# Graph attention layer: the values as two fp16 parts scaled per feature, in three products

## What is computed

```python
q = x @ wq.T + bq; k = x @ wk.T + bk; v = x @ wv.T + bv
q2, k2, v2 = (heads of q @ wiq.T + biq, k @ wik.T + bik, v @ wiv.T + biv)
mask = full(-inf); mask[src, dst] = softplus(w)[edge_type - 1]; # diagonal set where empty
scores = einsum('hnd,hmd->hnm', q2, k2) / 8 + mask
out = einsum('hnm,hmd->hnd', softmax(scores), v2)
return layernorm(x + (out @ wo.T + bo))
```

## Time and profile before

| | |
|---|---|
| median of 3 runs | 282.12 us (281.9 to 282.89) |
| the profiled execution | 282.69 us, span 280.9 us |
| TensorE, VectorE, ScalarE, GpSimd busy | 274.3, 174.6, 153.5, 137.1 us |
| value matmuls (L1025) | 240, busy 21.0 us |
| v2 stage ends, first attention step begins | 138.6 us |
| mean granted TensorE clock | 0.999 of full speed |

### The profile page before, as it was taken

One profiled execution on the slowest core, in us unless ns is written; L12 is line 12 of the kernel. 1 busy time (PEld: TensorE's weight loads), 2 busy tenths in 40 slices (PEclk: granted clock), 3 DMA queues, 4 the chain that ended last, 5 costly groups with the idle time before them and its releaser, 6 DMA issues.

```text
span 280.9 us, 5139 instructions
## 1 busy us (share of the span) xinstructions
PE 274.3 (98%) x1674; PEld 252.6 (90%) x1674; DVE 174.6 (62%) x425; ACT 153.5 (55%) x288; POOL 137.1 (49%) x123
## 2 busy tenths in 40 slices
PE   8999999999999999999999999999999999999992
PEld 8999999999999998888899989889898988787891
DVE  4879976765765676233506687857676577810472
ACT  5973343244244235233318989877879787933221
POOL 2000644565635555533697286483837466497000
PEclk9999999999999999999999999999999999999999
DMA  7949866274474335966404589795867849590032
GB/s 263 341 155 345 290 213 202 98 219 154 122 252 149 91 139 175 350 242 197 153 17 149 108 212 148 228 216 130 228 126 204 163 154 180 166 215 3 9 139 79
DMA packets 51921, 49.31 MB, mean 176 GB/s; under 512 B 41056, under 2 KB 41920, under 8 KB 51776
## 3 DMA queue, kind: packets, MB, share of 16 engines
q1 hardware_dynamic: 49792, 47.63, 58.4%
q0 software_dynamic: 1680, 0.62, 1.1%
q10 hardware_dynamic: 432, 0.85, 0.8%
HBM read 37.44 MB, written 2.21 MB: 141 GB/s over the span
## 4 chain that ended last, share of the span: by engine, by line
PE 98%; DVE 1%; ACT 0%; issue 0%
PE bank L928 24%; PE bank L919 19%; PE bank L921 19%; PE bank L920 19%; PE bank L1025 7%; PE bank L1007 5%; PE bank L944 3%; PE bank L937 1%; ACT res L606 0%; DVE stats L893 0%; DVE res L892 0%; DVE mean_var L895 0%; ACT std L601 0%; DVE scratch L623 0%; DVE rstd L898 0%
## 5 line engine op out<-in xcount | busy, mean ns | idle before, releaser
L387 POOL DMA_INDIRECT mask_cells<-scratch x48 | 53.8, 1120 | 72.1 <-DMA mask_cells<-scratch 29.6
L441 ACT ACTIVATE w_hi<-w_raw 128x1024 fp32r<-128x1024 f32 x49 | 51.5, 1053 | 22.2 <-PE bank L928 19.6
L349 POOL TENSOR_TENSOR w_lo<-w_raw,w_hi 128x1024 fp32r<-128x1024 f32 x17 | 40.8, 2404 | 39.9 <-DVE plane_lo_odd L826 30.4
L919 PE MATMUL bank<-x_hi,w_hi 128*128 128x384 f32 x176 | 58.8, 334 | 0.0
L920 PE MATMUL bank<-x_lo,w_hi 128*128 128x384 f32 x176 | 58.8, 334 | 0.0
L921 PE MATMUL bank<-x_hi,w_lo 128*128 128x384 f32 x176 | 58.8, 334 | 0.0
L633 DVE TENSOR_TENSOR w_lo<-w_raw,w_hi 128x1024 fp32r<-128x1024 f32 x31 | 37.9, 1225 | 16.6 <-ACT w_hi L441 15.6
L484 ACT ACTIVATE h_hi<-bank,bcol 128x384 f32 (+1 forms) x24 | 14.0, 582 | 55.4 <-PE bank L921 52.7
L919 PE MATMUL bank<-h_hi,w_hi 128*128 128x384 f32 x128 | 43.8, 342 | 0.0
L921 PE MATMUL bank<-h_hi,w_lo 128*128 128x384 f32 x128 | 42.8, 335 | 0.0
L920 PE MATMUL bank<-h_lo,w_hi 128*128 128x384 f32 x128 | 42.8, 334 | 0.0
(11 more groups left out here) (99 smaller groups left out, 443.1 us busy)
## 6 DMA issues: line engine op xcount, KB each, us to landing
w_raw<-weights SPq DMA_DIRECT2D x53, 512.0 KB
shared<-key_rows SPq DMA_DIRECT2D x6, 512.0 KB
shared<-start SPq DMA_DIRECT2D x5, 320.0 KB, 6.3
res<-x_rows SPq DMA_DIRECT2D x1, 1536.0 KB
out<-res SPq DMA_DIRECT2D x6, 256.0 KB, 2.2
mask_cells<-scratch POOLq DMA_INDIRECT x48
shared<-start ACTq DMA_DIRECT2D x2, 320.0 KB, 5.2
mask_cells<-mask SPq DMA_DIRECT2D x1, 576.0 KB, 6.0
```

The costliest lines, as they stand in the source:

```text
L349: nc.gpsimd.tensor_tensor(lo, w_raw[:, s, cols], hi.bitcast(F32), ALU.subtract)\
L387: nc.gpsimd.indirect_dma_start(out=mask_cells, out_offset=bass.IndirectOffsetOnAxis(ap=cell[:, c:c + 1], axis=0), in_=cell_value[:, c:c + ...
L441: nc.scalar.activation(w_part(t, s, slice(0, F))[0], w_raw[:, s, :], ACT.Copy).then_inc(w_hi_done, 1)
L919: pe.matmul(out_ps, w_hi[:, s, cols], moving_hi, start=(k == 0), stop=False)
```

## The change

The values are held as two fp16 parts instead of three bf16 parts, and the products are three: high plane by high and low part, low plane by high part. So that fp16 holds them, each feature (column of v2) is scaled: in step 0 ScalarE writes |v2| in bf16 (three Abs of 128 x 1024), TensorE sums them over the nodes in six matmuls with ones (behind the first k-slice of the k tile), VectorE reads from the sums the diagonal of each 128 x 128 block into `back` (eight operations) and scaled sums into `v_scale` (two), and after the evacuation of the k tile takes the reciprocal of all of `v_scale`. GpSimd multiplies the values of a pair by the scales (three multiplications), of pairs 0 and 1 in step 1, then one pair a step, and `v_low` is one subtraction. `att_high` and `att_low` scale by `back`. The high part of pair 0 is made at the start of step 2, no longer in step 1. In `softmax` exponentials 4 stand ahead of high plane 0, and planes 0 and 1 follow each other.

```diff
-        vp = sb("vp", [P, 2, NT, 2, 3 * D], BF16)
-        v_rest = sb("v_rest", [P, NT, P], F32)
+        vp = sb("vp", [P, 2, 2, NT, P], FP16)
+        v_scale = sb("v_scale", [P, F], F32)
+        back = sb("back", [P, KT], F32)
+        ones = sb("ones", [P, P], BF16)
...
+            def scale_values(a):
+                for n in range(NT):
+                    mine = v2[:, n, ds(a * P, P)]
+                    ins = nc.gpsimd.tensor_tensor(mine, mine, v_scale[:, ds(a * P, P)], ALU.mult)
+                ins.then_inc(v_scaled, 1)
             def v_low(a, par):
...
                 pool.wait_ge(vp_hi_done, a + 1)
...
+                nc.gpsimd.sem_inc(vp_hi_seen, 1)
+                nc.gpsimd.tensor_tensor(v_part(par, 1), v_pair(a), v_part(par, 0), ALU.subtract).then_inc(vp_done, 1)
...
+                elif isinstance(j, int) and j == 1:
+                    pool.wait_ge(scales_made, 1)
+                    scale_values(0)
+                    scale_values(1)
+                else:
+                    v_low(j - 1, 1 - par)
                 if not (isinstance(j, int) and j < 1):
-                    v_low(j - 1, 1 - par)
                     pool.wait_ge(plane_lo_done, 2 * NT * j)
...
+                if not last and not (isinstance(j, int) and j < 1):
+                    scale_values(j + 1)
             step(0, 0)
             step(1, 1)
+            v_low(0, 0)
...
+            def size(n):
+                act.wait_ge(v2_ready, 2 * n + 2)
+                nc.scalar.activation(v_size[n], v2[:, n, :], ACT.Abs).then_inc(sizes_made, 1)
             def v_high(a, par):
+                act.wait_ge(v_scaled, a + 1)
...
-                high_planes(a, (0,))
                 exps(a, (4,))
-                high_planes(a, (1,))
+                high_planes(a, range(0, 2))
                 exps(a, (5,))
...
+            def value_sums():
+                dve.wait_ge(sums_done, 1)
+                for k in range(KT):
+                    col = k * P % HALF
+                    ins = nc.vector.scalar_tensor_tensor(
+                        out=v_scale[:, k * P:(k + 1) * P], in0=size_bank[k * P // HALF][:, col:col + P],
+                        scalar=LEAST, in1=ident[:, :], op0=ALU.max, op1=ALU.mult, accum_out=back[:, k:k + 1])
+                then_settle(ins)
+                nc.vector.tensor_scalar(back[:, :], back[:, :], 1.0 / (FULL * UP), None, ALU.mult)\
+                    .then_inc(back_made, 1)
+                for h, half in enumerate(HALVES):
+                    ins = nc.vector.tensor_scalar(v_scale[:, half], size_bank[h][:, :], LEAST, 1.0 / FULL, ALU.max,
+                                                  ALU.mult)
+                ins.then_inc(sums_read, 1)
+            def value_scales():
+                dve.wait_ge(sums_read, 1)
+                nc.vector.reciprocal(v_scale[:, :], v_scale[:, :]).then_inc(scales_made, 1)
...
                     evacuate_pair(*q_tile)
+                    value_sums()
                     evacuate_pair(*k_tile)
+                    value_scales()
...
-                for z in range(3):
+                for z in range(2):
                     products(turned_hi, z, start=(z == 0))
...
-                for z in range(2):
-                    products(turned_lo, z, stop=(z == 1))
+                products(turned_lo, 0, stop=True)
+            def sum_sizes():
+                pe.wait_ge(sizes_made, NT)
+                for n in range(NT):
+                    for b, half in zip(size_bank, HALVES):
+                        ins = pe.matmul(b[:, :], ones[:, :], v_size[n][:, half], start=(n == 0), stop=(n == NT - 1))
+                ins.then_inc(sums_done, 1)
...
+                            if which == 1 and k == 0:
+                                sum_sizes()
                             continue
```

More of the change, by code:

```diff
@@ L65 @@
 UP = float(1 << 15)
+FULL = float(1 << 15)
+LEAST = 1e-25
 SCALE = 1.0 / 8.0
@@ L211, in gnn_layer @@
         v2_acc, v2_ready = sem("v2_acc"), sem("v2_ready")
-        vp_hi_done, vp_done = sem("vp_hi_done"), sem("vp_done")
+        sizes_made, sums_done, sums_read = sem("sizes_made"), sem("sums_done"), sem("sums_read")
+        scales_made, back_made = sem("scales_made"), sem("back_made")
+        v_scaled, vp_hi_done, vp_hi_seen, vp_done = (
+            sem(n) for n in ("v_scaled", "vp_hi_done", "vp_hi_seen", "vp_done"))
         scores_seen = sem("scores_seen")
@@ L396, in step @@
                 s0 = (2 * par + LEAD) % RING
+                last = isinstance(j, int) and j == PAIRS - 1
                 low_part(t + LEAD, s0)
@@ L402, in step @@
                         nc.gpsimd.tensor_tensor(res[:, n, :], res[:, n, :], bo_row, ALU.add).then_inc(res_ready, 1)
+                elif isinstance(j, int) and j == 1:
[4 more added lines that the diff above has]
+                    v_low(j - 1, 1 - par)
                 if not (isinstance(j, int) and j < 1):
-                    v_low(j - 1, 1 - par)
                     pool.wait_ge(plane_lo_done, 2 * NT * j)
-                if isinstance(j, int) and j == PAIRS - 1:
+                if last:
                     low_halves(t + LEAD + 1, s0 + 1)
@@ L551, in step @@
                 more = not (isinstance(j, int) and j < 2)
+                if not attend:
+                    size(0)
+                if isinstance(j, int) and j == 2:
+                    act.wait_ge(back_made, 1)
+                    v_high(0, 0)
                 split(t + LEAD, s0, raws)
-                if attend:
-                    if isinstance(j, int) and a == 0:
-                        act.wait_ge(v2_ready, 2 * NT)
+                if not attend:
+                    for n in range(1, NT):
+                        size(n)
+                if more:
                     v_high(a, 1 - par)
@@ L625, in _ @@
             nc.vector.memset(downs[:, :], 1.0 / UP)
+            nc.vector.memset(ones[:, :], 1.0)
             def low_part(t, s):
@@ L786, in att_low @@
                 nc.vector.scalar_tensor_tensor(
-                    out=att_lo[:, att, :].rearrange("p a n -> p (a n)"), in0=att_bank[:, 0:N], scalar=1.0 / UP,
+                    out=att_lo[:, att, :].rearrange("p a n -> p (a n)"), in0=att_bank[:, 0:N], scalar=back[:, att],
                     in1=att_hi[:, att, :].rearrange("p a n -> p (a n)").bitcast(F32),
```

30 lines of the change are left out of this document (10 added, 20 removed).

## The result

The changed kernel takes **284.85 us** (median of 5 runs, 284.53 to 285.41) against 282.14 us (281.9 to 282.89) for the kernel before: ratio 1.0087, 95% interval [1.0072, 1.0102]. It is slower by 0.9%. The forecast was 281.3, a gain of 0.8, with 277.6 to 283.6 as the range for eight times in ten. The result has the other sign, lies 3.5 us above the forecast and 1.2 above the upper end of the range.

What follows compares the result with a forecast made beforehand. TensorE, busy 98% of the span, was taken as the bound. -8.2 (value matmuls) + 1.56 (sums) + 2.3 + 1.3 + 1.5 + 0.3 + 0.4 (waits) = -0.8 us: 281.3 on the median, 277.6 to 283.6 eight times in ten.

Steps and rivals of the forecast that it cites:

- the slope of two tiny rows: Reciprocal of 128x1024 priced from rows of one and three elements, 164 and 177 ns: 6.5 ns per further element, 6.8 us.
- two of 0.66 = 4.3: VectorE's added work in step 0: eight 128x128 operations, a small one and two of 512 columns, 4.3 us in all.
- that cover is exactly used up: Step 0: after VectorE's added work the k low part begins at about 149.3 instead of 147.77, with no slack left.
- 0.3 of ScalarE's idle time: Before pair 2's scores: idle time ahead of 170.50 absorbs 0.3 of the chain's lateness; low attention part ends at 178.2.
- after that the two are together again and each step is 1.02 shorter: Steps behind the scores of pair 2: TensorE and the softmax chain level again, each step 1.02 us shorter.
- I expect nothing in the steady steps: Steady steps: the q low part comes 0.2 us short, and the reorder takes out that 0.2, so no loss.
- second sign of being wrong: TensorE timeline: gaps in every step, released by VectorE's q low part, would show the forecast wrong.
- third rival: ScalarE and VectorE set the steps from 4 on: +1.3 to +2 us, 282.6 to 283.3; chance 0.14.
- 0.3 for the change of pattern in step 4: Step 4: one loss of 0.3 us where the pattern changes, an estimate.
- 0.4 for pair 6's last transpose: Last pairs: pair 6's last transpose lands 14.4 us after T, wanted at 14.0; wait 0.4 us.
- rival that ended slower: Reciprocal costs more than the two tiny rows tell: at 9 ns an element 9.4 us, time 283.9; chance 0.08.
- short reciprocal: Reciprocal in step 0 streams one element a cycle, 1.2 us: -5.4, time 276.7 us; chance 0.10.

Runs made afterwards that it cites:

- e7: The changed kernel with 46 matmuls of 128 columns into an unused part of PSUM, filling TensorE's gap before step 2; 285.63 us.
- e12: The changed kernel with the scaling operation on the 128x8 table folded into the constant of the sums' matmuls; 284.31 us.
- e4: The kernel before with two reciprocals of 128x512, whose results nobody reads, ahead of the first mask of pair 0; 286.35 us.
- e1: The changed kernel without the scaling (no sums, reciprocal or GpSimd multiplications); three products and the new order of exponentials stay; 276.8 us.
- e2: The changed kernel with the reciprocal of 128x1024 replaced by one ordinary two-input VectorE operation; 280.52 us.
- e3: The changed kernel with the reciprocal cut up: 256 columns in step 0, then 128 columns for each later pair in VectorE's idle time; 279.52 us.
- e5: e3 with the small multiplication of `back` folded into the constant of the matmul with ones; 279.45 us.
- e9: The changed kernel with the query tile's evacuation, from step 3 on, ahead of the last two low planes (ScalarE: last two high planes); 285.17 us.
- e10: e5 with the query tile's evacuation ahead of low planes 4 and 5 from step 3 on; 278.53 us.
- e6: The changed kernel with GpSimd's operations on 1024 columns (weights' low parts, residual addition) cut into four of 256; 287.03 us.
- e8: The changed kernel with the old order of exponentials and high planes (plane 0 ahead of exponentials 4); 288.24 us.

## Why the prediction was wrong

On the aligned clock TensorE stands this late against the kernel before, forecast and seen (T is the start of a pair's scores):

| place | forecast | seen |
|---|---|---|
| T of pair 0 | 1.6 | 1.3 |
| T of pair 1 | 5.2 | 5.3 |
| T of pair 2 | 5.7 | 6.5 |
| T of pair 3 | 4.6 | 6.5 |
| T of pair 4 | 3.9 | 5.85 |
| T of pair 6 | 1.9 | 4.4 |
| T of pair 7 | 0.9 | 3.8 |
| end of the span | -0.8 | +2.0 |

The row for pair 3 uses the chain of the kernel before:

```profile
185.61 1.77 PE bank L1007 x18
```

**Right: the mechanism up to pair 2.** The reciprocal took 6.54 us for 6.8 forecast; the slope of two tiny rows held for this size. The sums are on the chain with no wait ahead and cost 0.3 less than forecast. Step 2's q tile waited 2.69 for 2.3; the scores of pair 1 waited 1.1 for 1.3 in the runs that kept the clock (e7, e12); the scores of pair 2 waited 1.56 for 1.5. e4 reproduced the stall in the kernel before. Value matmuls take 1.60 for 18, as forecast (1.54). The Trainium skill ("VectorE: DVE Perf Modes", section "First, the fixed hardware budget") gives the reciprocal a repeat count of 8. Read as 8 cycles an element at the page's 0.96 GHz, that was an estimate of 8.5 us; the trace gives 6.25 ns an element, 6 such cycles.

**Wrong, 0.8 us up to pair 2: "two of 0.66 = 4.3" and "that cover is exactly used up".** The small operation on 128x8, priced at next to nothing, took 2.21. The eight reads ahead of it took 1.8 us where I had put their upper bound, 2.8, which happened to hide half of that; so the k part's evacuation came 0.66 late, at 149.96 on the aligned clock for 149.3; the shorter reciprocal took part of that back, and the chain behind it is 6.7 late for 6.5. In its profiled run e12 gives 0.9 us back by taking the operation out. The rest is the path from there to the low attention part: it ended 6.7 late, for 6.0. I had let it recover 0.3 of ScalarE's idle time. The 0.42 ahead of the evacuation of the k part did go, but ScalarE now waits 0.96 for pair 1's second inverse sums, where it waited 0.51: VectorE reaches the low planes later behind the new order, and needs 2.11 us for the first two instead of 1.90, beside GpSimd's subtraction.

**Wrong, 1.0 us in step 3: "after that the two are together again and each step is 1.02 shorter".** The step of pair 2 to pair 3 gave nothing (13.07 for 12.04). An operation on three elements (L862) was held for 1.50 us behind GpSimd's weight part, and the q tile then waited 0.70 for VectorE. In e1 the same operation took 0.86 at that place, behind `v_low`, and the q tile waited 0.33. The length of the step follows the end of this operation: 4.72 after T of pair 2 in e1, whose step lasts 12.74, and 5.06 to 5.08 after T in e2, e3, e5, e7, e12 and the changed kernel, whose steps all last 13.07 to 13.10, although the operation lasts anything from 1.14 to 1.51 there. The 0.35 between them goes with GpSimd's multiplications by the scales, which stand ahead of the weight part and which the forecast had put at nothing; the other 0.7 is lost without any scaling. No run changed this operation alone, but e9 and e10, which take the q tile's evacuation out from behind this chain, win 0.8 and 1.0 in this step. A shown wait of 0.70 cost more than that: the next matmul stands 1.04 after the last one instead of 0.17, and the one after that 0.28 instead of 0.17, 0.98 in all.

**Wrong, 1.1 us in steps 4 to 7: "I expect nothing in the steady steps".** I had found the margin to be 0.2 too short and let the reorder give it back exactly. It did: the q low part ended 9.97 - 0.2 = 9.77 after T by the forecast and does so in the trace (200.80 + 0.61 - 191.64). Still the steps last 12.17 us, not 11.87. What failed is the step from a margin of zero to a cost of zero. In the step behind, the part ended at 213.60 where TensorE, at its pace of 0.17, would have gone on at 213.51; but its next two matmuls stand 0.31 and 0.29 behind the ones before them instead of 0.17, so that 0.26 us went for a part that was 0.09 late. Here the gaps come in every step, released by VectorE's q low part, which was my second sign of being wrong. It is the place of the third rival, to which I had given 0.14, though that rival named another cause (a reorder that brings nothing, or longer planes) and ended at 283.3 at most. The chain shows the place, 201.46 0.44 where its neighbours have 0.17. e1 has the same period without scaling, so it belongs to the faster value products and not to the added work. Where e9 and e10 take the wait away, two of their steps last 11.9 to 12.0 and the others lose it again to the transposes and GpSimd, which stand a few tenths behind. The margin was to be read as a limit common to several engines, not as zero. The 0.3 for the change of pattern in step 4 and the 0.4 for pair 6's last transpose were not seen as such (step 4 lasts 12.20, and the values of pair 6 follow their scores at once, at 241.55): without these two terms the forecast would have been 0.7 lower, and further off.

**Wrong, 0.6 us outside the span:** the forecast took that part for constant. It is, within a program, but not between these two.

0.8 + 1.0 + 1.1 - 0.1 (the tail) = 2.8 in the span, and 0.6 outside: 3.4 of the 3.5. The rival that ended slower blamed a longer reciprocal; it was refuted by its row. The short reciprocal was refuted as well, but e2 shows that its forecast for that case, 276.7, would have failed too: 280.5 was measured, with an operation of 1.77 us in the reciprocal's place, and 0.65 of it outside the span.

## What to carry to other kernels

An instruction on the path of a chain costs by where it stands: of 1024 reciprocals in one instruction ahead of a softmax chain, 768 were taken away and cut in pieces into idle time, where they cost nothing visible, and that gave 4.7 us back. When the bound engine gets faster by 1 us a step, ask for each engine behind it how far it stands from the new period, and count a margin near zero as a loss of some 0.3 us in every step, as here; an edit worth nothing before (the exponentials' order) can be worth 3.4 us after. On VectorE the length of a tiny operation on SBUF operands can be set by what GpSimd is running, so such an operation on the path is worth folding away (e12, by its profile).

## What the runs showed of the hardware

- **VectorE behind GpSimd.** TENSOR_SCALAR of 128x8: 2.21 us beside GpSimd operations of 2.4 us, 0.41 beside operations of a quarter of the columns and 0.7 us. TENSOR_TENSOR of 128x3: 0.15 to 1.50 us. The long ones end with a GpSimd instruction. The Trainium skill states this rule in "SBUF — State Buffer", section "SBUF: two separate sides": a VectorE operation in one of its two-port modes, or with two SBUF inputs where the GpSimd operation reads SBUF, and a GpSimd operation exclude each other for a whole instruction. The trace agrees at both places (ends 0.04 and 0.02 us apart), and the reciprocal, which has one SBUF input, ran beside GpSimd's weight parts (from 148.26, 4.78 us for two) without lengthening them or being held. I had not applied it to operations so small.
- **RECIPROCAL** costs 6.25 ns an element of a partition, and about 0.14 us: 0.94 us for 128 columns, 1.74 for 256, 6.54 for 1024.
- **A short wait of TensorE** costs more than it shows: 0.26 us for a low part 0.09 late, and 0.98 for a shown wait of 0.70.
- **The granted clock** fell to its lower level about 1 us after TensorE had come back from 2.69 us of idle time, and stayed there for some 3.5 us. It fell in the same way behind gaps of 2.31, 1.85 and 2.69 us in the profiled runs of e4, e6 and e9, and not in those of e8 and e12, whose gaps were 2.68 and 1.85 us, so the length of the gap alone does not decide it. By e7 and e8 it cost nothing here.
- **Outside the span** lie 1.7 to 1.85 us in some of these programs and 2.4 to 2.5 in others, and 1.95 in e6, the same to 0.15 in every run of one program. This stays open.
